# Preparing the first scan chunk inside the convolution, and beginning the first tap transfers in the sources stage

## The reference

```python
def _L0_conv_ref(x, W_in, conv_w, conv_b, x_proj_w, dt_proj_w, dt_proj_b, A_logs, Ds, ln_w, ln_b, W_out):
    ...   # group norm, projection W_in, depthwise 3x3 convolution, SiLU: u in four scan orders
    def _selective_scan(u, delta, A, Bm, Cm, D, delta_bias):
        ...
        delta = jax.nn.softplus(delta + delta_bias[None, :, None])
        def step(h, inp):
            ut, dt, bt, ct = inp
            dA = jnp.exp(dt[..., None] * A4)
            h = dA * h + (dt * ut)[..., None] * bt[:, :, None, :]
            y = jnp.einsum('bkdn,bkn->bkd', h, ct)
            return (h, y)
        ...
        return y + u * D[None, :, None]
    ...   # sum over four directions, layer norm, gate, W_out, residual
def _compute_spectral(u, sigma, phi, Mpp, Mpm):
    U_plus, U_minus = _stu_conv(phi, u, PADDED_SL)     # causal convolution with 16 filters phi
    s = sigma ** SIGMA_POW
    out = jnp.einsum('btkd,k,kde->bte', U_plus, s, Mpp)
    out = out + jnp.einsum('btkd,k,kde->bte', U_minus, s, Mpm)
    return out
```

## Time and profile before

| what | us |
|---|---|
| median of 3 runs | 6189.54 |
| lowest and highest run | 6186.34, 6195.12 |
| the profiled execution, its own time | 6196.9 |
| its span | 6195.1 |
| PE busy | 5676.1 (92%) |
| DVE busy | 4384.0 (71%) |
| ACT busy | 3169.3 (51%) |
| POOL busy | 3095.3 (50%) |

### The profile page before, as it was taken

How to read it: one execution, slowest core, us unless ns; L and a number is a source line. 1 busy time by engine, 2 the same in 40 slices (tenths; PEclk the granted TensorE clock), 3 DMA queues, 4 the chain that set the end, 5 groups by cost and what they waited for, 6 DMA issues and landing times. The chain is left out here.

```text
span 6195.1 us, 128742 instructions
## 1 busy us (share of the span) xinstructions
PE 5676.1 (92%) x41691; PEld 5066.6 (82%) x41691; DVE 4384.0 (71%) x5986; ACT 3169.3 (51%) x6029; POOL 3095.3 (50%) x2015
## 2 busy tenths in 40 slices
PE   7899999999888999999998667999999989999998
PEld 5688888888766888888886546999989879999987
DVE  2699999999717999999996664555555555555554
ACT  2699888988737998899886321111111111111110
POOL 1699999999717999999996301111111101111110
PEclk9899999999998999999999888999999999999999
DMA  2455555555414555555554237777766666777765
GB/s 97 109 145 141 141 140 142 140 145 141 128 60 121 143 145 139 139 144 144 142 141 123 56 99 173 156 152 151 152 153 154 167 152 149 154 155 159 153 151 146
DMA packets 1098946, 858.33 MB, mean 139 GB/s; under 512 B 305622, under 2 KB 1021238, under 8 KB 1064374
## 3 DMA queue, kind: packets, MB, share of 16 engines
q1 hardware_dynamic: 1097974, 844.72, 55.1%
q10 hardware_dynamic: 720, 10.49, 0.4%
HBM read 811.50 MB, written 43.55 MB: 138 GB/s over the span
## 5 line engine op out<-in xcount | busy, mean ns | idle before, releaser
L726 POOL TENSOR_TENSOR read<-state,c_wide 128x1024 f32<-128x1024 f32 x1024 | 2419.9, 2380 | 216.7 <-DVE state L762 129.0
L762 DVE TENSOR_TENSOR_SCAN state<-decay,carry,p_drive 128x512 f32<-128x512 f32 x1792 | 2140.9, 1259 | 103.9 <-PE p_drive L540 57.1
L658 ACT ACTIVATE decay<-step,a_neg 128x512 f32<-128x512 f32 x2048 | 1398.2, 717 | 225.1 <-DVE state L762 215.9
L1747 PE MATMUL p_y<-window,x_high 128*128 128x256 f32 x7936 | 1490.8, 286 | 0.0
L1811 ACT COPY term_blocks<-p_s 128x256 f32<-128x256 f32 x832 | 310.5, 373 | 2096.2 <-PE p_s L1747 2096.2
L1747 PEld LDWEIGHTS p_y<-window,x_high 128*128 128x128 f32 x7936 | 1239.1, 191 | 0.0
L1747 PE MATMUL p_y<-window,x_low 128*128 128x256 f32 x3968 | 1130.5, 285 | 0.0
L553 PE MATMUL p_y<-ident,read 128*128 128x128 f32 x8192 | 1064.1, 273 | 13.0 <-ACT y_tok L672 3.7
L542 PE MATMUL p_drive<-diag_b,xu_tok 128*128 128x128 f32 x8192 | 1004.0, 276 | 1.3 <-DVE state L762 1.3
L542 PEld LDWEIGHTS p_drive<-diag_b,xu_tok 128*128 128x128 f32 x8192 | 960.5, 193 | 1.6 <-DVE state L762 1.6
L553 PEld LDWEIGHTS p_y<-ident,read 128*128 128x128 f32 x8192 | 925.2, 141 | 25.4 <-issue 21.7
(11 more groups left out here) (257 smaller groups left out, 6023.7 us busy)
## 6 DMA issues: line engine op xcount, KB each, us to landing
c_wide<-c_scratch SPq DMA_DIRECT2D x256, 1024.0 KB, 4.7
window<-taps_scratch SPq DMA_DIRECT2D x576, 257.0 KB, 6.5
diag_b<-diag_scratch SPq DMA_DIRECT2D x256, 512.0 KB, 4.1
window<-taps_scratch SPq DMA_DIRECT2D x768, 129.0 KB, 5.3
window<-taps_scratch SPq DMA_DIRECT2D x128, 513.0 KB, 7.1
window<-taps_scratch SPq DMA_DIRECT2D x64, 385.0 KB, 6.1
gate_scratch<-gate_out SPq DMA_DIRECT2D x16, 512.0 KB, 3.1
gate_in<-gate_scratch SPq DMA_DIRECT2D x8, 1024.0 KB, 6.0
```

Of the source, the lines that this page charges most:

```text
L658: act.activation(decay[:, n % 2, t, :], step[:, c.parity, t, :], ACT.Exp, scale=m.a_neg[:, DT2 * c.k + t, n:n + 1]).then_inc(s["decay"], 1)
L726: pool.tensor_tensor(read[:, n % 4, :, :], state[:, n % 4, :, :], wide, ALU.mult).then_inc(s["read_out"], 1)
L762: dve.tensor_tensor_scan(flip(state[:, n % 4, t, :], c), flip(decay[:, n % 2, t, :], c), flip(p_drive[:, n % 2, t, :], c), 0.0 if c.start ...
L1747: last = pe.matmul(out, x[:, source, blk, :], view[:, :, at:at + P][:, :, ::-1], start=first and x is m.x_high and z == 0, stop=True, skip ...
```

## The change

Three things are done.

The first chunk's preparation moves into the convolution. The steps become methods of a class `Preparation`, with the same instructions and waits as before, and are called after certain of the 16 units: `project` and `keep_projection` after unit 5, `step_product` and `step_parts` after 6, `turn_b`, `keep_b`, `step_exp`, `step_ln` after 7, `turn_x` and `keep_x` after 11 and 12, `store_rows`, `finish_step` and `step_times_u` after `g == 1`. The loops over `g` are written out. The tiles of the preparation are now allocated outside the blocks (`chunk_ready`; the image tokens and the gate's buffers share their room with them), and so are two PSUM banks (`p_prep`, `p_b`). `begin_y` is replaced by `add_second`, which does the part of a channel tile that a `g` makes possible; its parts for `g` of 0, 1 and 2 stand in the convolution on DVE, and that for 3 at the head of `scans`.

The first load of window `a` moves from the head of `filter_and_mix` to `sources`, behind the two token loads; its tile is now allocated around both blocks.

SP no longer waits in `sources` for the landing of the stores; ACT waits for them in `filter_and_mix` where it reads them back.

```diff
@@ convolution @@
+        prep, chunk = Preparation(m), Chunk(b, 0, 0, 0, 0, first=True)
-            with sp.Fori(0, NG) as g:
+            for g in range(NG):
...
+                if g == 1:
+                    prep.store_rows(sp, nc, chunk)
...
-            with pool.Fori(0, NG) as g:
+            for g in range(NG):
...
+                                       ALU.mult).then_inc(m.sem_b["y_begun"], 1)
+                if g == 1:
+                    prep.step_times_u(pool, chunk)
...
-            with pe.Fori(0, NG) as g:
+            for g in range(NG):
...
                         last.then_inc(s["gate_mm"], 1)
+                        unit = 4 * g + 2 * half + t
+                        if unit == 5:
+                            pe.wait_ge(s["gated"], START + b * 17 + 5)
+                            prep.project(pe, chunk)
+                        if unit == 6:
+                            prep.step_product(pe, chunk, 0)
+                            prep.step_product(pe, chunk, 1)
+                        if unit == 7:
+                            prep.turn_b(pe, chunk)
+                        if unit in (11, 12):
+                            prep.turn_x(pe, chunk, unit - 11)
...
-            with act.Fori(0, NG) as g:
+            for g in range(NG):
...
+                        if unit == 5:
+                            prep.keep_projection(act, chunk)
+                        if unit == 6:
+                            prep.step_parts(act, chunk)
+                        if unit == 7:
+                            prep.keep_b(act, chunk)
+                            act.preload_act_table_set("natural_log_exp_and_others")
+                            prep.step_exp(act, chunk)
+                            prep.step_ln(act, chunk)
+                        if unit in (11, 12):
+                            prep.keep_x(act, chunk, unit - 11)
...
+            for g in range(NG - 1):
+                for t in range(DT2):
+                    dve.wait_ge(s["gated"], START + b * 17 + g * 4 + (4 + t))
+                    dve.wait_ge(m.sem_b["y_begun"], START + b * 8 + (2 * g + t + 1))
+                    add_second(dve, m, g, t)
+                if g == 1:
+                    prep.finish_step(dve, chunk)
...
+def add_second(dve, m, g, t):
+
+    y = m.y[:, t, :].rearrange("p (h w) -> p w h", w=W)
+    x = m.s2[:, t, :].rearrange("p (w h) -> p w h", h=H)
+    new, past = slice(WIN * g, WIN * (g + 1)), slice(0, WIN * g)
+    last = g == NCH // 2 - 1
+    pieces = [(slice(0, W), new)] if last else []
+    for w in range(0, W, WIN):
+        pieces.append((slice(w + 4 * g, w + 4 * g + 4), past if last else slice(0, WIN * (g + 1))))
+        if g and not last:
+            pieces.append((slice(w, w + 4 * g), new))
+    for columns, rows in pieces:
+        ins = dve.scalar_tensor_tensor(y[:, columns, rows], x[:, columns, rows], m.d_skip[:, 10 + t:11 + t],
+                                       y[:, columns, rows], ALU.mult, ALU.add)
+    return ins
...
@@ scans @@
                 if c.first:
-                    store_rows(c)
                     sp.wait_ge(s["c_stored"], START + c.g * 32 + 32)
...
                 if c.first:
-                    project(c)
-                    step_product(c, 0)
-                    step_product(c, 1)
-                    turn_b(c)
-                    turn_x(c, 0)
-                    turn_x(c, 1)
                     drive(c, 0)
                     drive(c, 1)
...
                 if c.first:
-                    keep_projection(c)
-                    step_parts(c)
-                    keep_b(c)
-                    step_exp(c)
-                    step_ln(c)
-                    keep_x(c, 0)
-                    keep_x(c, 1)
                     times_b(c, 0)
...
-                if c.first:
-                    step_times_u(c)
...
                 if c.first:
-                    begin_y(0)
-                    finish_step(c)
-                    begin_y(1)
+                    for t in range(DT2):
+                        add_second(dve, m, 3, t).then_inc(s["y_whole"], 1)
@@ sources @@
+            load_windows(sp, m, "a", 0)
             sp.wait_ge(past_kept, 8)
             sp.dma_start(m.past_dram[0], past[:, :, :]).then_inc(past_out, 16)
...
             sp.dma_start(m.past_dram[1], past[:, :, :]).then_inc(past_out, 16)
-            sp.wait_ge(past_out, 16 * NB)
-            sp.wait_ge(u_out, 32)
@@ filter_and_mix @@
-            load("a", 0)
             load("b", 0)
             load_m(0)
             load("c", 0)
...
+            act.wait_ge(m.past_out, 16 * NB)
             act.dma_start(m.acc[:, :, :], m.past_dram[0]).then_inc(s["acc_in"], 16)
             filters(act, 0, body)
             act.wait_ge(s["joined"], START + KF * SLOTS)
+            act.wait_ge(m.u_out, 32)
             act.dma_start(blocks[:, 0:2 * BASE, :], m.u_dram.rearrange("p s j c -> p (s j) c")).then_inc(s["u_in"], 16)
```

307 lines of the change are left out of this document (167 added, 140 removed).

## The result

The changed kernel takes 6160.90 us, median of 5 runs (6159.94 to 6164.62), the kernel before beside it 6189.96 (6186.34 to 6195.12): ratio 0.9953, 95% interval 0.9938 to 0.9967. That is 29.1 us less, inside the range of 6130 to 6164 by 3 us, but 19 us above the forecast of 6142. The two profiled executions differ by 35.1 us (spans 6195.1 and 6160.0). Where these lie is read by cutting both spans at the same events: first and last product of the convolution, first and last scan of a batch, last product of `sources`, slot 12 of the first filter.

The account below looks back on a forecast made before the run. Bounds: PE in the convolution, a preparation chain at the head of `scans`, window `x`'s arrival at slot 12 in the filter. 44.7 - 11.2 + 3.0 + 10.9 = 47.4 us off 6189.54 gives 6142 us, range 6130 to 6164.

Parts of the forecast that it names:

- Part 1, the head of `scans`: Head of `scans`: the 63.1 us wait before the first scans shrinks to 9.2 us a batch, gaining 44.7 us.
- Part 2, PE's added work: Convolution: the preparation's products and transposes moved onto PE cost 5.6 us a batch, 11.2 us lost.
- Part 2, PE waits for nobody: Convolution: PE's waits for helpers cost 0; rival, PE stands 13.8 us longer a batch, 6170 us, chance 0.07.
- DVE's pieces ... 0: Convolution: DVE's pieces of `y` for `g` 0 to 2 fit in its idle time and cost 0.
- The written-out loops: 0: Convolution: writing out the loops over `g` costs 0, as straight code is fetched ahead.
- Part 3, the ramp: First scans: PE's `project` for the second chunk moves ahead of the first scan, 1.5 us a batch, gain 3.0 us.
- Part 4, the filter's head: Head of `filter_and_mix`: 1.8 us from the earlier start plus 9.1 from window `a` leaving the queue, 10.9 us gained.
- the rival in which the store and window `b` give it back: Filter's head: 2 MB store and window `b` share engines, part 4 gives 1.8 us or less; 6151 us, chance 0.10.
- The starved PE: Convolution: written-out units each begin with 2.85 us of PE idleness, 91 us over 32 units; 6233 us, chance 0.03.
- The sum: Whole kernel: 44.7 - 11.2 + 3.0 + 10.9 = 47.4 us gained, giving 6142 us; forecast's chance 0.75.

Follow-up runs that it names:

- 64 memsets: Changed kernel with 64 one-column memsets in DVE's wait inside the convolution, behind the last `keep_low`: 6153.85 us, ratio 0.9920.
- the edit alone: Kernel before with only the filter's part (window `a` issued in `sources`, waits for stores moved): 6185.15 us, ratio 0.9991.
- the moved load of `acc`: Changed kernel with 64 memsets, the filter's first load of `acc` issued behind ACT's copy of slot 12: 6153.44 us, ratio 0.9921.
- 74 after the change: Changed kernel with 74 one-column memsets in DVE's idle time in the convolution: 6157.75 us, ratio 0.9948.
- 128 before it: Kernel before with 128 one-column memsets in DVE's idle time in the convolution: 6192.41 us, ratio 1.0005.

## Why the prediction was right, and by how much it wasn't

- **Part 1, the head of `scans`**: 44.7 us forecast, 46.7 found. The ten pieces were put at 9.2 us and took 8.4. ACT's operand for the first state was ready before DVE was, as said.
- **Part 2, PE's added work**: 5.6 us a batch forecast. Where the clock doesn't fall on the way the convolution takes 121.3 to 122.2 us instead of 116.3 to 117.5, 4.7 us more between the means, so the products cost somewhat less than forecast. In one batch the clock falls behind the step products, and the convolution is 1.7 to 2.7 us longer than the other of the same execution; I had taken 0.99 from the earlier trace rows for the whole stretch and kept the lower clock only as a bound. The fall of the changed kernel's profile is in batch 1.
- **Part 2, PE waits for nobody**: right. PE is busy for 123.89 of 123.89 us, and ACT, with 0.61 us to spare behind unit 8 instead of 5.0, was the nearest to it. That rival is out. The added pieces on DVE are 40 in the convolution (4, 8 and 8 for each tile), not the 36 that the prediction counted, and it doesn't matter there.
- **"DVE's pieces ... 0" and "The written-out loops: 0"**: this is the step that failed, a cost that was put at nothing, and it is three quarters of the miss. The pieces do cost nothing where they are executed. Their cost is in their number: 54 more instructions in DVE's program shift the four chunk loops behind them, and two of these then branch back in 3.7 to 4.6 us instead of 0.3. That is 13.8 us of lengthened chunks in the profile, and 13.2 us between the medians with 0 and with 64 memsets. I had cited the Trainium skill (Runtime: NRT & Kernel Launch, "Instruction fetch mechanics") for straight code being fetched ahead and a taken branch out of the window being slow, and weighed only its first half, on the loops that were written out. Its second half bore on the loops that stayed. By that rule a loop can stall at its branch back or not by where it lies; the runs agree that the place decides, but whether the slow branches are those whose target is out of the window no run here shows.
- **Part 3, the ramp**: 3.0 us forecast. Where no loop stands the scans are 2.4 us shorter, but that the numbers are near is luck. PE's `project` did move, from 4.0 us behind the first scan to 0.6 and 1.0 us ahead of it. Of the ramp itself only 1.0 us is gone, both of its lengths (63.9 us and 65.4 to 66.9) occur in the kernel before as well, and the rest comes from the end of the batch, of which part 3 says nothing. What sets the length of the ramp is open.
- **Part 4, the filter's head**: 10.9 us forecast, 11.1 found at slot 12 and 11.4 with the edit alone, split 3.3 and 7.8 rather than 1.8 and 9.1. For slot 4 the prediction read a landing as the end of the wait where the earlier trace rows has "issue"; the sum doesn't rest on it. At slot 12 the rival in which the store and window `b` give it back is out; in the time of the edit alone (0 to 11 us less) it isn't excluded.
- **The starved PE**: out as well, no idle time of PE in 32 written-out units.
- **The sum**: 47.4 us forecast. Found against forecast, by the table at the top: head of the scans +2.0, convolution -1.1, scans -14.0, filter's head +0.2, the stretches between -5.7. That makes 28.8 us, against 29.1 between the medians, and of the 18.6 us missed 14 are in the scans, where the branches stand; the 5.7 of the stretches between lie within what these vary by from run to run. The range held by luck: it had been stretched for the filter's rival, not for this.

## What to carry to other kernels

An instruction that is hidden where it runs still moves all code behind it on its engine. Where loops follow, look at the time from each branch back to the instruction behind it, per engine, before and after; if it has gone from 0.3 to 4 us, a few dozen idle instructions ahead of the loops (here 64) may bring back more than the edit that one was about to try (here 13 us, where the moved load of `acc` brought nothing that could be told), and a comparison of two kernels that differ in code ahead of a loop should be made at more than one shift.

When an expected gain is missing and every engine has the same work as before, compare the period of the steady state chunk by chunk: lengthened periods at a fixed rhythm point to the loop, not to the data.

## What the runs showed of the hardware that I had not expected

- 54 memsets of one column made a kernel of 6191 us 23 us slower, and 64 of them made another one 13 us faster. Only DVE's branches were touched; those of ACT, POOL, PE and SP took 0.1 to 0.4 us in every kernel. Which places are slow stays open: the count of instructions from the program gives two kernels the same place (74 after the change, 128 before it), of which one has a slow loop and the other none.
- A wait of DVE at such a branch is put down to PE's product in the profile ("2.17 <-PE p_drive L656"), though that was there in time at the same point of the next chunk.
- Four products of 8 rows in a row (2.1 us) were followed by 3 to 4 us at the lower clock in one of two batches, in eight of nine profiles: where they began 54.42 us or more behind the convolution's first product, and never where they began at 54.24 or less.
- Five strided DVE operations took 4.24 us alone and 6.54 beside POOL's products.
